# Shared expert's down products in 256-column halves, its activations 64 bytes further

## What is computed

```python
x = x + 0.5 * ffn(layernorm(x))
x = x + mamba(layernorm(x))      # residual inside as well
x = x + 0.5 * ffn(layernorm(x))

# ffn: 64 routed experts (top 4, at most 64 tokens each, hidden 128) plus two shared experts, 2 x 512 hidden
sg = einsum('nd,sfd->nsf', flat, sh_gate_w)
su = einsum('nd,sfd->nsf', flat, sh_up_w)
out = out + einsum('nsf,sdf->nd', silu(sg) * su, sh_down_w)
```

## Time and profile before

| | before |
|---|---|
| median of 3 runs | 2303.09 us (2301.91 to 2306.98) |
| profiled execution | 2305.35 us |
| its span in the trace | 2303.6 us |
| PE busy | 2252.9 us, 98% |
| weight loads on PE | 2003.2 us, 87% |
| DVE, ACT, POOL busy | 1363.3, 882.4, 693.7 us |
| granted PE clock, mean | 0.995 |

### The profile page before, as it was taken

One profiled execution on the slowest core, in us unless ns is written; L12 is line 12 of the kernel. 1 busy time (PEld: TensorE's weight loads), 2 busy tenths in 40 slices (PEclk: granted clock), 3 DMA queues, 4 the chain that ended last, 5 costly groups with the idle time before them and its releaser, 6 DMA issues.

```text
span 2303.6 us, 41271 instructions
## 1 busy us (share of the span) xinstructions
PE 2252.9 (98%) x16412; PEld 2003.2 (87%) x16412; DVE 1363.3 (59%) x3201; ACT 882.4 (38%) x1563; POOL 693.7 (30%) x534
## 2 busy tenths in 40 slices
PE   6999999999998999999999999999999999999998
PEld 6999998777798899999998999998999999777787
DVE  6777762222228677777777777778777763223322
ACT  5232321233327555554555555455323231223321
POOL 1244443112220433233332223331144444122222
PEclk9999999999999999999999999999999999999999
DMA  8776525989844111111111111104376532988949
GB/s 273 263 260 209 164 84 181 306 282 284 236 89 138 45 30 36 28 28 29 28 28 29 28 28 29 28 22 169 125 282 224 199 104 78 312 291 286 290 83 183
DMA packets 129279, 334.73 MB, mean 145 GB/s; under 512 B 24450, under 2 KB 45186, under 8 KB 118400
## 3 DMA queue, kind: packets, MB, share of 16 engines
q1 hardware_dynamic: 80592, 236.63, 28.7%
q0 software_dynamic: 48496, 95.46, 18.1%
HBM read 218.25 MB, written 172.77 MB: 170 GB/s over the span
## 4 chain that ended last, share of the span: by engine, by line
PE 87%; DVE 4%; ACT 4%; DMA 3%; issue 1%; SPq 0%; DVEq 0%; POOL 0%; ACTq 0%; POOLq 0%
PE m_p_ab L1687 3%; PE m_p_x L1687 3%; PE m_p_x L1689 3%; PE m_p_x L1688 3%; PE m_p_ab L1689 3%; PE m_p_ab L1688 3%; PE p_up_b L769 3%; PE p_x_b L873 3%; PE p_x_a L873 3%; PE p_up_a L769 3%; PE p_gate_b L769 2%; PE m_p_y L1808 2%; PE m_p_y L1809 2%; PE p_up_b L771 2%; PE p_up_b L770 2%; PE p_gate_b L770 2%
## 5 line engine op out<-in xcount | busy, mean ns | idle before, releaser
L2004 DVE SCALAR_TENSOR_TENSOR m_xt<-m_ssm,m_convw,m_xt 128x256 f32<-128x256 f32 x384 | 211.9, 565 | 55.2 <-ACT m_ssm L1553 46.0
L1687 PE MATMUL m_p_ab<-m_ht_hi,m_wi_b_hi 128*128 128x256 f32 x576 | 164.5, 286 | 3.8 <-ACT m_ssm L1553 3.4
L506 POOL DMA_INDIRECT slot_rows<-a_hr,a_slot_now x128 | 128.4, 1003 | 131.3 <-PE p_gate_a L771 81.0
L506 POOL DMA_INDIRECT slot_rows<-b_hr,b_slot_now x128 | 128.9, 1007 | 129.5 <-PE p_gate_b L771 80.1
L1688 PE MATMUL m_p_ab<-m_ht_lo,m_wi_b_hi 128*128 128x256 f32 x576 | 161.3, 280 | 0.0
L1689 PE MATMUL m_p_ab<-m_ht_hi,m_wi_b_lo 128*128 128x256 f32 x576 | 161.2, 280 | 0.0
L769 PE MATMUL p_gate_a<-a_hts_hi,a_w_hi 128*128 128x256 f32 x512 | 148.4, 290 | 1.8 <-DVE a_hts_lo L1068 1.8
L1457 POOL TENSOR_TENSOR m_state_dec<-m_state,m_etot 128x1024 f32<-128x1024 f32 x31 | 74.0, 2386 | 248.7 <-ACT m_etot L1569 248.7
L769 PE MATMUL p_gate_b<-b_hts_hi,b_w_hi 128*128 128x256 f32 x512 | 147.0, 287 | 0.3 <-DVE b_hts_lo L1068 0.3
L769 PE MATMUL p_up_a<-a_hts_hi,a_w_hi 128*128 128x256 f32 x512 | 145.5, 284 | 0.0
L769 PE MATMUL p_up_b<-b_hts_hi,b_w_hi 128*128 128x256 f32 x512 | 145.4, 284 | 0.0
(11 more groups left out here) (378 smaller groups left out, 7346.7 us busy)
## 6 DMA issues: line engine op xcount, KB each, us to landing
a_ew<-in_ew SPq DMA_DIRECT2D x32, 1536.0 KB, 7.2
b_ew<-in_ew SPq DMA_DIRECT2D x32, 1536.0 KB, 7.3
after_ffn<-a_zeros POOLq DMA_DIRECT2D x6, 2048.0 KB, 9.2
out<-b_zeros POOLq DMA_DIRECT2D x6, 2048.0 KB, 10.1
slot_rows<-a_zeros POOLq DMA_DIRECT2D x1, 8336.0 KB, 37.1
a_rows<-slot_rows SPq DMA_DIRECT2D x32, 260.5 KB, 8.4
b_rows<-slot_rows SPq DMA_DIRECT2D x32, 260.5 KB, 8.2
m_x<-after_ffn SPq DMA_DIRECT2D x16, 512.0 KB, 3.6
```

The lines of the kernel that those rows point to most:

```text
L506: g_.indirect_dma_start(out=xg, out_offset=bass.IndirectOffsetOnAxis(ap=slot_now[r % HR][:, at:at + 1], axis=0), in_=hr[r % HR][:, j, :], ...
L1687: t.matmul(out, l_hi, r_hi_, start=first, stop=False)
L2004: ins_ = v.scalar_tensor_tensor(xt[:, m, :], ssm[:, m, i:i + BM], convw[:, m, i:i + 1], xt[:, m, :], ALU.mult, ALU.add)
```

## The change

Where a 512-column matmul stood in `down`, two of 256 columns stand, one for each half of `p_out`'s bank. The order is now: the three products of the first half, then the three of the second. The one exception is the very first product of a bank (n == 0, in the down call of u = 0), which stays 512 wide, with `start=True`. A down call of u = 0 so has 2 matmuls of 512 and 20 of 256 columns, each other call 24 of 256: (22 + 3 x 24) x 16 x 2 = 3008 matmuls instead of 1536, 1472 more.

`act_hi` and `act_lo` start 64 bytes past a multiple of 256. `var_eps` moves in front of them (it fills the gap). In the state-space part `xdt`, `xs`, `state` and `la` move up by 128 bytes, so that nothing lies over `var_eps`.

```diff
-        act_hi, act_lo = sb("act_hi", [P, 2, 2, BS], F32R, w_at), sb("act_lo", [P, 2, 2, BS], F32R, w_at)
+        var_eps = sb("var_eps", [P, TILES])
+        act_hi, act_lo = sb("act_hi", [P, 2, 2, BS], F32R, w_at, LINE // 4), sb("act_lo", [P, 2, 2, BS], F32R, w_at, LINE // 4)
         silu, prod = sb("silu", [P, 2, 2, BS]), sb("prod", [P, 2, 2, BS])
         mv = sb("mv", [P, TILES, 2])
-        var_eps, rstd, neg_mean = sb("var_eps", [P, TILES]), sb("rstd", [P, TILES]), sb("neg_mean", [P, TILES])
+        rstd, neg_mean = sb("rstd", [P, TILES]), sb("neg_mean", [P, TILES])
...
                     for j in range(TS):
                         tok = slice(j * P, (j + 1) * P)
-                        mm = three(p_out[:, j, :], act_hi[:, i % 2, m, tok], act_lo[:, i % 2, m, tok],
-                                   wd(w_hi)[:, n, :], wd(w_lo)[:, n, :], n == 0, n == CF - 1)
+                        hi, lo = act_hi[:, i % 2, m, tok], act_lo[:, i % 2, m, tok]
+                        if n == 0:
+
+                            t.matmul(p_out[:, j, :], hi, wd(w_hi)[:, n, :], start=True, stop=False)
+                        for half in range(2):
+                            cols = slice(half * (D // 2), (half + 1) * (D // 2))
+                            out, last = p_out[:, j, cols], n == CF - 1 and half == 1
+                            if n > 0:
+                                t.matmul(out, hi, wd(w_hi)[:, n, cols], start=False, stop=False)
+                            t.matmul(out, hi, wd(w_lo)[:, n, cols], start=False, stop=False)
+                            mm = t.matmul(out, lo, wd(w_hi)[:, n, cols], start=False, stop=last)
                 mm.then_inc(down_done, 1)
...
         cdec, decay = [cdec_both[:, j, :, :] for j in range(TM)], [decay_both[:, j, :, :] for j in range(TM)]
+        sb.next += 4 * TILES
         xdt_both = sb("xdt", [P, TM, NH, HP])
```

## The result

| | before | after |
|---|---|---|
| median of 22 runs each, one chip | 2302.69 us | 2306.61 us |
| lowest to highest | 2299.86 to 2315.39 us | 2302.70 to 2318.56 us |
| ratio, 95% interval | | 1.0024 [1.0013, 1.0034] |
| runs over 2310 us | 1 of 22 | 8 of 22 |
| profiled execution, its span | 2305.35, 2303.6 us | 2315.7, 2313.7 us |

The change makes the kernel slower by 3.9 us in the median; I had forecast 5.4 us faster. Two things have to be kept apart. The lowest runs differ by 2.8 us, and after has many more runs in an upper group, some 10 us above the rest. The profiled execution of after belongs to that upper group.

The account below looks back on a forecast made before the run. PE bounds the kernel, through the distance between matmul starts. Terms -11.7 + 3.1 + 1.5 + 1.7 = -5.4 us gave 2299.95 us for the profiled execution, 2297.7 us for the median; range 2291.5 to 2316.

Parts of the forecast that it names:

- the zero for the state-space part: State-space products with `xdt` and `state` moved: place makes no difference to 128-column products, zero; ends +-4.7 us.
- the 64 bytes make short halves possible: Down: moving weights 64 bytes before the activations, as in gate and up, allow 113.3 ns between halves instead of 117.9.
- What the down call hands on: Gate and up directly behind down: 2544 matmuls turn from long to short rhythm, 4.6 ns each, -11.7 us at most.
- Rival B: Passage from down to gate, operands level, sets the long rhythm: down short, gate long, no gain, about 2307 us; chance 0.20.
- gate and up (-11.7 + 3.1): Gate and up behind down: -11.7 us from short rhythm, 3.1 missing where slow up products behind logits keep it long.
- down: 14 calls behind logits, openers (1.5 + 1.7): Down: 14 calls continuing the slow rhythm from the logits pay 1.5 us; 64 opening 512-column matmuls pay 1.7 us.
- Splitting at zero: Down's 1472 split matmuls: in short rhythm a pair takes 226.6 ns, nothing lost; in long rhythm 13.4 us more.
- The openers: The 64 opening down matmuls left 512 wide: each disturbs seven matmuls by 3.8 ns, 27 ns, 1.7 us in all.
- the upper bound that I had named: Openers: all matmuls behind them up to the next break in the long rhythm, another 2 to 4 us.
- No wait and no semaphore is added: Weight loads and queues: no added wait or semaphore, `down_done` once per call; extra loads' cost is in the distances.
- costed POOL's queue at nothing: Queues: SP's and POOL's orders don't change; POOL works with slack, zero.

Follow-up runs that it names:

- e1: The kernel before with down in halves as in the change, nothing moved, so both operands level: 2315.04 us, ratio 1.0028 to before.
- e4: The kernel before with the down weights moved to 64 bytes before a multiple of 256, activations unmoved, down in halves: 2313.57 us, ratio 1.0018 to before.
- e9: The kernel before with each whole-block add to the accumulator in DRAM moving only 16 of 512 columns: 2301.80 us, ratio 0.9983 to before.
- e10: The changed kernel with each whole-block add to the accumulator in DRAM moving only 16 of 512 columns: 2303.61 us, ratio 0.9990 to before.
- e6: The changed kernel with the 64 opening 512-column matmuls of down in halves too: 2309.75 us, ratio 1.0031 to before.
- e11: The kernel before with four buffers instead of five between the experts' products and the scatter-adds: 2321.81 us, ratio 1.0067 to before.
- e5: The changed kernel run again, unaltered, beside before on one chip: 2310.02 us against 2303.28, ratio 1.0024.
- e8: e7 plus the last three matmuls of each state-space output product in halves: 2294.22 us, ratio 0.9960 to before.
- e7: The kernel before with only the last three matmuls split, in the 60 down calls that gate follows directly: 2301.25 us, ratio 0.9986 to before.
- e12: e8 with only the very last matmul of a down call or output product in two halves: 2302.23 us, ratio 0.9971 to before.
- e2: The changed kernel's places with down in 512 columns again: 2307.26 us, ratio 0.9988 to before.
- e3: The kernel before with only the down weights moved, to 64 bytes before a multiple of 256, down in 512 columns: 2311.61 us, ratio 1.0005 to before.

## Why the prediction was wrong

The place that bounds the kernel was right: PE, and the distance between starts. So were the count of matmuls, the zero for the state-space part, and that the 64 bytes make short halves possible (e1 against after).

**The step that failed is "What the down call hands on".** I took a short run to stay short until something breaks it, so that a short down call would hand on the short rhythm. From the earlier trace rows I had that a 512-column run hands on the long one whatever came before it, and I put it down to the width. The runs show instead that the rhythm ahead and the places at the passage together set the rhythm behind it, and that in after the passage turns it: behind a short down call gate is long, 34 times of 34. So gate and up gave 3.2 us, where I had put 11.7 less 3.1. In after, gate follows the halves with the moving and the stationary operand both in the weights, level, and the rhythm is turned over; up hands to down with `hts` (192 past a multiple of 256) moving and `act` (64 past) loaded, and it is turned over again, in 29 of 34 calls without openers. In e4, where each passage has the relation that the products have, it is kept. Rival B had the right place, the level pair at the passage, but the wrong effect: it sets nothing long, it inverts. Whether it is the relation at the passage that counts, or that operands change their places there, is open, and so is the cause behind either: that the load of one matmul's operand and the stream of the one before it share something by their addresses would fit, but the runs show the pattern, not that.

The terms, forecast and as measured between before and after (in brackets e9 and e10):

| term | forecast | measured |
|---|---|---|
| gate and up (-11.7 + 3.1) | -8.6 us | -3.2 (-2.9) |
| down: 14 calls behind logits, openers (1.5 + 1.7) | +3.2 us | +5.6 (+6.0) |
| sum | -5.4 us | +2.4 (+3.1) |
| of it rhythm | -5.4 us | +1.1 (+1.8) |
| of it the wait for `a_htr_lo` | none | +1.6 (+1.2) |
| late stretch | none | 10 us, in some 4 of 10 runs |

**Splitting at zero** failed with it: over half of the halves are long (1546 distances of 2943), since each short up product turns the down call behind it long. With the openers down's rhythm costs 4.5 us where I had 3.2. **The openers** were mis-sized: I gave each seven disturbed matmuls, 27 ns; they set the whole rest of the call long, the upper bound that I had named, but e6 shows that only 12 of the 32 calls would be short without them. For the time it mattered little.

**"No wait and no semaphore is added" was true and not enough.** Waits that were there grew: the one for `a_htr_lo` by 1.6 us, and the chain of adds came to hold PE up. The chain of adds on POOL's queue has little slack in before too (e11: one buffer less and it fails once in each part), and how far a block add of 512 KB lies behind a load of an expert's weights changed with PE's timing (3.0 us in before, 0.5 in after, though the units start only about 1 us later). I had costed POOL's queue at nothing because its order doesn't change; that its meetings in time move was not in the forecast. With the small block adds the upper group of runs goes (0 of 12 against 6 of 12 in e5), and the distance between the two kernels falls from 3.9 us (the result) and 6.7 (e5) to 1.8 (e10 against e9). The cause of the upper group is so far shown. That it needs a meeting with a weight load is not: in e8 a block add at 503.4 us is issued 0.6 us behind such a load, the next issue waits 10.2 us for it, nearly as long as in after, and PE waits for nothing there. What else has to come together stays open.

The result, 2306.61, lies inside the range and beside rival B's 2307, for another reason than B's: that is luck, and the range was wide. The Trainium skill (TensorE: Matmul & The Clock Gate, Back-to-back issue gap) puts the gap of a single warm matmul at N / 2.4 + 2.5 ns, from which a split costs 2.5 ns and the change 3.7 us, as an estimate. The clean difference of 1.8 to 2.9 us is nearer to that than my -5.4; still the rule doesn't describe what happens, as no distance of 109 or 216 ns occurs, the halves' own come in 113.3, 117.9 and 120, and in e1 the same split costs down 17.2 us.

## What to carry to other kernels

When matmuls run back to back, compare the distance between starts for each relation of the places of the two operands, and look at the passages between products too: what one product hands to the next may be worth more than anything within it, and it can be had by splitting just its last three matmuls (e7, e8) or its last one (e12). Check then what the whole gains: e7 alone can't be told from before, e8 and e12 can. Don't take a rhythm seen in one place to carry over to another order of places without a run that has that passage. And where a chain of dependent DMAs has a few microseconds of slack, a change of PE's timing needs the spread of many runs, not one profile: here the profiled executions are 10 us apart and the medians 4.

## What the runs showed of the hardware that was not expected

- A run of 256-column float32r matmuls has one of two distances, 113.3 or 117.9 ns, where the moving operand lies 64 bytes before the stationary one modulo 256, and about 120 ns where the two are level (e1). For 512 columns it is the other way round: 226.7 ns level, 233 ns with the 64 bytes (e2, e3).
- A passage where the places stand in the same relation keeps the rhythm (59 of 60 in e4); in after, where the relation at the passage is another one and the operands' places change, it is inverted (59 of 60 between down and gate, 58 of 60 in e5; 29 of 34 between up and down).
- Two split halves, distances 113 and 119 ns, are enough ahead of a passage to make 48 matmuls behind it short (e12, 58 of 60).
- 7 us of standing still cost 8 to 10 us (10.2 in after, 16.7 for two in e11): PE's granted clock falls to 1.2 GHz during the wait, 2.5 us into it in after, and stays there for 10.2 us in after, 6.8 in e5.
- A DMA of the router, issued near 108 us in all kernels, takes 9.6 to 9.8 us in the six kernels with halves in all down calls and 8.0 to 8.3 us in the eight others; the cause is open.
